# Depthwise convolution of the query tiles: from quad passes, VectorE and GpSimd taps to one phase-split pass on TensorE

## The reference

```python
# layer 0: linear attention over q, k, v and a second set of them out of two grouped convolutions
qkv = concat(h @ wq.T, h @ wk.T, h @ wv.T)             # 768 channels
dw = conv(qkv, dw_kernel, 5x5, one filter per channel)  # depthwise, SAME
pw = conv(dw, pw_kernel, 1x1, groups of 8 channels)
f = concat(qkv, pw) as heads of 3 x 8 channels          # query, key, value
query, key = relu(f[q]), relu(f[k])
scores = einsum(value with a row of ones, key)          # summed over the pixels
out = einsum(scores, query); out = out[:-1] / (out[-1:] + EPS)
x = batchnorm(conv1x1(out, proj_kernel)) + x
# layer 1: softmax attention over 1024 pixels, keys and queries from the normalised image
x = conv1x1(softmax(F(norm x) . G(norm x)) @ H(x)) + x
```

## Time and profile before

| | before |
|---|---|
| median of 3 runs | 660.25 us (659.42 to 661.57) |
| profiled execution, its own time | 659.5 us |
| span, first to last instruction | 657.6 us |
| mean granted TensorE clock | 0.99 |
| PE, DVE, POOL, ACT busy | 617.1, 523.6, 494.3, 473.5 us |

### The profile page before, as it was taken

How to read it: one execution, slowest core, us unless ns; L and a number is a source line. 1 busy time by engine, 2 the same in 40 slices (tenths; PEclk the granted TensorE clock), 3 DMA queues, 4 the chain that set the end, 5 groups by cost and what they waited for, 6 DMA issues and landing times.

```text
span 657.6 us, 13133 instructions
## 1 busy us (share of the span) xinstructions
PE 617.1 (94%) x5448; PEld 445.1 (68%) x5448; DVE 523.6 (80%) x616; ACT 473.5 (72%) x772; POOL 494.3 (75%) x236
## 2 busy tenths in 40 slices
PE   5979989989899999999899999999999999899997
PEld 3845466647678876556578876557568875367897
DVE  4999895878869798977789999879889996264543
ACT  4698689877759798987786988888777786243331
POOL 4579879976998999977999899959989997013000
PEclk9989999999999999999999999999989999999999
DMA  8000000101100000001100000000100000000000
GB/s 318 9 1 4 2 2 2 64 2 64 65 1 17 21 30 1 1 2 64 65 1 17 16 18 17 3 1 1 65 0 17 16 18 18 0 1 1 16 17 33
DMA packets 6698, 16.67 MB, mean 25 GB/s; under 512 B 880, under 2 KB 1136, under 8 KB 6128
## 3 DMA queue, kind: packets, MB, share of 16 engines
q1 hardware_dynamic: 6640, 15.84, 6.7%
HBM read 11.64 MB, written 4.19 MB: 24 GB/s over the span
## 4 chain that ended last, share of the span: by engine, by line
PE 80%; DVE 11%; ACT 5%; issue 2%; DMA 1%; SPq 0%; DVEq 0%; ACTq 0%
PE ps L786 12%; PE ps L762 12%; PE ps L597 7%; PE ps L877 5%; PE ps L531 5%; PE ps L535 4%; PE ps L532 4%; PE ps L777 4%; DVE ps L1365 3%; PE ps L843 2%; PE ps L635 2%; PE ps L810 2%; PE ps L731 2%; PE ps L605 2%; DVE small L1545 2%
## 5 line engine op out<-in xcount | busy, mean ns | idle before, releaser
L1626 POOL TENSOR_TENSOR conv<-conv,prod 128x930 f32<-128x930 f32 (+4 forms) x174 | 382.1, 2239 | 48.3 <-ACT prod L1068 45.5
L1365 DVE SCALAR_TENSOR_TENSOR ps<-raw,dw_sb,ps 128x930 f32<-128x930 f32 (+4 forms) x264 | 317.2, 1202 | 6.5
L1068 ACT ACTIVATE prod<-raw,dw_sb 128x961 f32<-128x961 f32 (+4 forms) x209 | 217.2, 1100 | 0.7 <-POOL q_raw L1626 0.7
L786 PE MATMUL ps<-ht,pt 128*128 128x256 f32 x384 | 86.4, 379 | 0.0
L1255 ACT ACTIVATE rows<-ps,small 128x1024 f32<-128x1024 f32 x32 | 35.7, 1115 | 69.2 <-DVE small L1550 69.1
L786 PEld LDWEIGHTS ps<-ht,pt 128*128 128x128 f32 x384 | 71.3, 190 | 8.9
L1626 POOL TENSOR_TENSOR rows<-rows,prod 128x930 f32<-128x930 f32 (+4 forms) x26 | 58.2, 2240 | 7.5 <-ACT prod L1068 4.3
L1545 DVE TENSOR_REDUCE small<-ps 128x1 f32<-128x1024 f32 x32 | 39.1, 1222 | 20.3 <-PE ps L762 20.3
L762 PE MATMUL ps<-hi,t_hi 128*128 128x512 f32 x128 | 45.3, 436 | 5.0 <-ACT rows L1255 5.0
L762 PE MATMUL ps<-lo,t_hi 128*128 128x512 f32 x128 | 41.2, 404 | 0.0
L531 PE MATMUL ps<-hi,wqkv_hi 128*128 128x512 f32 x92 | 38.7, 421 | 2.3 <-ACT t_sums L1099 1.5
(11 more groups left out here) (185 smaller groups left out, 1163.2 us busy)
## 6 DMA issues: line engine op xcount, KB each, us to landing
q_raw<-x_dram SPq DMA_DIRECT2D x8, 512.0 KB, 5.4
x<-x_dram SPq DMA_DIRECT2D x4, 1024.0 KB, 4.7
out_dram<-x_t SPq DMA_DIRECT2D x16, 256.0 KB, 2.0
conv<-wqkv_dram SPq DMA_DIRECT2D x1, 768.0 KB, 4.3
conv<-fg_dram SPq DMA_DIRECT2D x1, 512.0 KB, 5.9
proj_sb<-proj_dram SPq DMA_DIRECT2D x1, 512.0 KB, 7.4
pw_sb<-pw_dram SPq DMA_DIRECT2D x1, 384.0 KB, 6.6
mask_sb<-masks_dram SPq DMA_DIRECT2D x1, 280.0 KB, 6.2
```

Source lines behind the costliest of these rows:

```text
L786: mm = pe.matmul(dst[:, 0:C], pt[:, i % PT_BUFS, j, :], ht[:, j, :], start=(j == 0), stop=(j == NB - 1))
L1068: act.activation(dst, view, ACT.Copy, scale=weight(t, i)).then_inc(prod_ready, 1)
L1365: return dve.scalar_tensor_tensor(dst, view, w, before, ALU.mult, ALU.add)
L1626: pool.tensor_tensor(total, total, product, ALU.add).then_inc(conv_pool, 1)
```

## The change

The two query tiles leave DVE, ACT and POOL: their depthwise convolution is done whole on PE, in one pass an image, `phase_conv`. The image is split into four phases (even and odd rows by even and odd columns) of 16 x 16 pixels with a border of one. A 5x5 filter over the image is, phase by phase, a sum over nine offsets of the phase images. 8 channels x 4 phases make the 32 rows of a tile, so one 32*32 weight does all taps of one offset for 8 channels and all four output phases; four channel groups (`g`) are the column groups and four units (`r`) the row groups. A wave is sixteen 32*32 matmuls with 256 columns; there are 2 tiles x 9 offsets = 18 waves, and both tiles' sums share the four banks.

ACT writes the raw queries into `stage` by phase (two copies of 256 elements in place of one of 512). Sixteen DMAs move them so that the phases of a channel lie in neighbouring partitions (`load_phases`, SBUF to SBUF, 32 partitions x 2 pieces each), into the place where `t_hi` and `t_lo` lie later; the tables of the weights lie beside them and in `pt` and are loaded again for each image (`load_taps`). For the next image `phase_conv` stands behind `output_weights(b, 1)`; for image 0 in the prologue between the two spreads of the denominators. ACT's `phase_sums` empties the four banks. The pointwise step of the queries is by phase: for each of four units eight 128*32 matmuls with 256 columns, and ACT's relu puts the pixels back in order. `shared_quads`, `first_quads(2)` and `(3)`, the lates, POOL's part of tile 1, DVE's taps of tile 0 and the weight products for tiles 0 and 1 go. `PROD_BUFS` is 4 and the `TAPS_` and `PRODUCTS_` tables, `RSTD_AT` (where POOL's two powers stand among the adds) and the tables of the prologue have new numbers.

```diff
-LATE_OF = (9, 10, 10, 10)
-SHARED_OF = (0, 3, 3, 3)
-QUAD_OF = (16, 12, 12, 12)
-FIRST_QUAD_TAPS = 12
-PROD_BUFS = 5
+LATE_OF = (0, 0, 0, 0)
+SHARED_OF = (0, 0, 0, 0)
+PHASES = 4
+PSIDE = SIDE // 2 + 2
+PIMG = PSIDE * PSIDE
+OFFSETS = [(ey, ex) for ey in (-1, 0, 1) for ex in (-1, 0, 1)]
+PROD_BUFS = 4
...
-    return own + [(SHARED_TILE, i) for i in SHARED_REST[b][LATE_OF[b] + SHARED_OF[b]:]]
+    return [(t, i) for t in (2, 3) for i in TAP_RANGE]
...
-TAPS_PROJ = ((1, 0, 1, 0, 1, 0, 1, 1), (1, 0, 1, 0, 1, 0, 0, 0), (1, 0, 1, 0, 1, 0, 1, 1))
-TAPS_STAT = (1, 0, 0)
+TAPS_PROJ = ((1, 0, 1, 0, 1, 0, 0, 7), (1, 0, 0, 0, 0, 0, 0, 6), (1, 0, 0, 0, 0, 0, 1, 5))
+TAPS_STAT = (3, 4, 1)
...
-FIRST_SPLIT = 24
+FIRST_SPLIT = 19
...
-            a_end = lay_out(A_AT, [("sums_0", QUADS), ("pwkv", A_PWKV), ("sums_1", QUADS)], b_, a_end)
+            a_end = lay_out(A_AT, [("pwkv", A_PWKV)], b_, a_end)
...
-            a_end = lay_out(A_AT, [("mb_raw", nx)], b_ + 1, a_end)
+            a_end = lay_out(A_AT, [("mb_raw", nx), ("sums", QUADS * nx)], b_ + 1, a_end)
...
+            def load_taps():
+                for t in range(CK):
+                    sp.dma_start(tap_weights[t], taps_phases[t]).then_inc(taps_loaded, 16)
+
+            def load_phases(b):
+                sp.wait_ge(a_free, A_RQ[b][-1] + 1)
+                for f in range(PHASES):
+                    for g in range(QUADS):
+                        sp.dma_start(phased[f::PHASES, :, g, :], stage[g::QUADS, :, f, :]).then_inc(phases_loaded, 16)
...
             for b in range(B):
+                if b + 1 < B:
+                    if b == 0:
+                        sp.wait_ge(a_full, A_AT["sums", 0] + QUADS)
+                    load_taps()
+                    load_phases(b + 1)
                 if b + 2 < B:
                     sp.wait_ge(d_full, D_AT["proj", b] + D_PROJ)
                     load_x(b + 2)
...
+            def phase_conv(b):
+
+                pe.wait_ge(taps_loaded, 16 * CK * (b + 1))
+                pe.wait_ge(phases_loaded, 16 * PHASES * QUADS * (b + 1))
+                for t in range(CK):
+                    for e, (ey, ex) in enumerate(OFFSETS):
+                        for r in range(QUADS):
+                            k = slice(r * QUAD, (r + 1) * QUAD)
+                            bank = a_slot(A_AT["sums", b] + r) if t == e == 0 else a_bank(A_AT["sums", b] + r)
+                            for g in range(QUADS):
+                                view = phased_img[k, t, g, 1 + ey:PSIDE - 1 + ey, 1 + ex:PSIDE - 1 + ex]
+                                mm = pe.matmul(bank[g * QUAD:(g + 1) * QUAD, t * QUARTER:(t + 1) * QUARTER],
+                                               tap_weights[t][k, e, g, :], view,
+                                               start=(e == 0), stop=(e == len(OFFSETS) - 1))
+                mm.then_inc(a_full, QUADS)
...
+                dst = a_slot(A_AT["pwq", b] + 2 * t + h)
+                if t == h == 0:
+                    pe.wait_ge(pw_phases_loaded, 16)
+                    pe.wait_ge(a_free, A_AT["sums", b] + QUADS)
+                for x in range(2):
+                    for r in range(QUADS):
+                        mm = pe.matmul(dst[r * QUAD:(r + 1) * QUAD, x * QUARTER:(x + 1) * QUARTER],
+                                       pw_ph[:, t, r, 2 * h + x, :], conv_ph[:, t, r, :], start=True, stop=True)
                 mm.then_inc(a_full, 1)
...
             def body(b):
                 with_next = b + 1 < B
-                shared_quads(b, 0)
...
-                shared_quads(b, 1)
                 if with_next:
                     raw_kv(b + 1)
...
                 output_weights(b, 1)
+                if with_next:
+                    phase_conv(b + 1)
...
-            first_quads(2)
             first_whole(1)
             fused_weights(A_AT["mb_raw", 0], A_AT["st_raw", 0], 0)
             spread_denominators(D_AT["bc_raw", 0], 1, 0)
-            first_quads(3)
+            phase_conv(0)
...
+                    for y in range(2):
+                        mm = act.copy(stage_img[:, t, 2 * y:2 * y + 2, rows_at, 1:PSIDE - 1],
+                                      src.rearrange("p (a y c x) -> p y x a c", y=2, c=SIDE // 2, x=2)[:, y])
...
+            def phase_sums(b):
+
+                slot = A_AT["sums", b]
+                act.wait_ge(a_full, slot + QUADS)
+                for r in range(QUADS):
+                    act.copy(conv_ph[:, :, r, :], a_bank(slot + r).rearrange("p (t n) -> p t n", t=CK)).then_inc(a_free, 1)
...
                     fused_weights(A_AT["mb_raw", b + 1], 0)
+                    phase_sums(b + 1)
                 x1_transposes(b, 3)
...
-                    pool.wait_ge(d_full, D_AT["proj", b] + D_PROJ)
-                    quad_products(pool, later_weights, SHARED_TILE, QUAD_OF[b + 1]).then_inc(quad_weights_ready, 1)
```

More of the change, by code:

```diff
@@ L75 @@
 CARRY = (0, 0, 0, 0)
[L78 to L82, removed]
+LATE_SEQ = [[] for _ in range(B)]
 def pool_order(b):
[L87 to L90, removed]
+    return [(t, i) for i in TAP_RANGE for t in (POOL_TILES if b else FIRST_POOL_TILES)]
 def dve_order(b):
-    own = [(t, i) for t in (2, 3, 0) for i in TAP_RANGE if b or t or i not in FIRST_QUAD_SEQ]
-    return own + [(SHARED_TILE, i) for i in SHARED_REST[b][LATE_OF[b] + SHARED_OF[b]:]]
+    return [(t, i) for t in (2, 3) for i in TAP_RANGE]
 POOL_SEQ = [pool_order(b) for b in range(B)]
 DVE_SEQ = [dve_order(b) for b in range(B)]
-POOL_STARTS = [[(t, 0) for t in POOL_TILES] + SHARED_SEQ[b][:1] for b in range(B)]
+POOL_STARTS = [[(t, 0) for t in POOL_TILES] for b in range(B)]
 ADD_SEQ = [[tap for tap in POOL_SEQ[b] if tap not in POOL_STARTS[b]] for b in range(B)]
@@ L141 @@
[L141 to L147, removed]
@@ L611, in first_quads @@
                 t, h = QUAD_UNITS[n]
[L612 to L613 removed]
+                quads(A_AT[f"first_{n}", 0], t, h, list(TAP_RANGE), first_weights)
             def first_whole(h):
@@ L619, in first_whole @@
                 whole(dst, lambda r: quad_ident, h, True).then_inc(a_full, 1)
-            def shared_quads(b, h):
-                pe.wait_ge(a_free, A_RQ[b][-1] + 1)
-                pe.wait_ge(quad_weights_ready, b + 1)
-                quads(A_AT[f"sums_{h}", b], SHARED_TILE, h, QUAD_SEQ[b], later_weights if b else first_weights[SHARED_TILE])
-            def queries(b, t, h):
-                dst, cols, late = a_slot(A_AT["pwq", b] + 2 * t + h), slice(h * HALF, (h + 1) * HALF), t == SHARED_TILE
-                own = any(tap[0] == t for tap in DVE_SEQ[b] + POOL_SEQ[b])
-                last = [tap for tap in DVE_SEQ[b] if tap[0] == t][-1:]
-                if h == 0 and last:
-                    pe.wait_ge(conv_dve, dve_count(b, DVE_SEQ[b].index(last[0]) + 1))
-                if own:
-                    mm = pe.matmul(dst, pw_sb[:, t, :], conv[:, t, cols], start=True, stop=(b > 0 and not late))
-                if late and LATE_SEQ[b]:
-                    if h == 0:
-                        pe.wait_ge(conv_pool, late_add_count(b, late_adds_of(b)))
-                    pe.matmul(dst, pw_sb[:, t, :], late_of[b][:, cols], start=not own, stop=False)
-                if late or b == 0:
-                    if h == 0 and not late:
-                        pe.wait_ge(pw_quads_loaded, 16)
-                    pe.wait_ge(a_free, (A_AT[f"sums_{h}", b] if late else A_AT[f"first_{2 + h}", b]) + QUADS)
-                    mm = whole(dst, lambda r: pw_quad[:, t, r, :], h + (2 if late and b == 0 else 0),
-                               not own and not (late and LATE_SEQ[b]))
@@ L842, in body @@
                         if t < 2 * CK:
-                            pe.matmul(dst[:, c0:c0 + P], block, pw_sb[:, t, :], start=True, stop=True)
+                            pe.matmul(dst[:, c0:c0 + P], block, pw_sb[:, t - CK, :], start=True, stop=True)
                         else:
@@ L1381, in conv_taps @@
                     before = None if starts else acc
-                    if t == SHARED_TILE and starts and SHARED_OF[b]:
-                        before = final
-                        dve.wait_ge(conv_pool, add_count(b, len(ADD_SEQ[b])))
                     tap(final if i == NTAPS - 1 else acc, t, i, before).then_inc(conv_dve, 1)
```

152 lines of the change are left out of this document (89 added, 63 removed).

## The result

| | before | after |
|---|---|---|
| median | 660.33 us (4 runs, 659.42 to 661.57) | 671.01 us (4 runs, 667.36 to 672.43) |
| ratio | | 1.0169 [1.0144, 1.0194] |
| profiled execution / its span | 659.5 / 657.6 us | 667.36 / 665.6 us |
| mean granted TensorE clock | 0.99 | 0.976 |

The forecast was 651, the range 641 to 668.

What follows compares the result with a forecast made beforehand. PE's own sequence was taken as the bound: 659.5 - 5.8 - 26.6 (quad passes) - 15.0 (queries) + 38.4 (three later phase_convs) = 650.5, so 651 us as the median against 660.25; range 641 to 668.

Steps and rivals of the forecast that it cites:

- Instruction supply: In phase_conv: 100 matmul records and loads a us, near the quads' 64, so instruction fetches cost nothing in the sum.
- Both signs of being wrong: Listed among the signs of a wrong forecast: phase_conv over 13.8 us, and gaps with "issue" inside it.
- a mis-sized term: phase_conv's 18 waves at 0.64 us each, 11.5 us a call, with 8.0 and 11.9 at the ends.
- The start of image 0's pointwise step: L843 in image 0, at 86.16 before: taken as unchanged, with PE back near 75.0 + 11.5 = 86.5.
- The quad passes: Shared tile's passes on PE's path, removed: 5.8 us saved in image 0, 26.6 in images 1 to 3.
- the queries of image 0: Pointwise step of the queries: four units in 4.0 us for 8.2 before, 4.2 us saved in image 0.
- the phases were in time: Sixteen DMAs of load_phases before phase_conv: costed at nothing, the phases being wanted 27 us after the last query row.
- Starvation of POOL: Behind phase_conv: 2.5 us of POOL idle, hidden as long as POOL has the room of the removed adds.
- all else: Quad passes and queries of images 1 to 3, beyond image 0: PE gives up 37.4 us.
- Fetch stalls: Rival, chance 0.13: each phase_conv crosses 4.6 fetches at 0.86 us, growing by 4.0 us; 16 in four images, 667.
- Paced by their count: Rival, chance 0.08: tile matmuls cost 31 ns a record whatever their columns, phase_conv 18.0 us, 677 in all.
- The other rivals: POOL late for L843 (0.10, 658.7); relief of DVE, POOL and ACT pays (0.09, 644); phases land late (0.04, 666).

Runs made afterwards that it cites:

- e1: The changed kernel with half the columns in every matmul of phase_conv and as many instructions (part of the convolution left out): 675.93 us.
- e3: The changed kernel with the fold's spread and last two fused weights moved inside the later phase_convs, ACT's fold and DVE's taps moved too: 657.23 us, 0.9982 to before.
- e7: The changed kernel with five of nine offsets in phase_conv, ten waves in place of eighteen (convolution not whole): 644.82 us.
- e2: The changed kernel with four of ACT's five products among image 0's raw queries moved behind them: 670.09 us, ratio 1.0178 to before.
- e6: The changed kernel with prologue edits alone: products behind raw queries, denominators' scores after 34 DVE taps for 39, second spread inside phase_conv(0): 666.80 us, 1.0133 to before.

## Why the prediction was wrong

**The step that failed** is "Instruction supply ... I value this at nothing in the sum". It chose the right suspect (the waits in L656) and argued it away by an average rate: phase_conv's 100 instructions a us were called nearer to the quads' 64 than to the 197 of L656. The limit lies between them: one block of 256 in 3.45 us is 74 a us. At the quads' 31 ns a record the 128 matmul records of a block take 4.0 us, an estimate from the earlier trace rows, so the next block is there in time. Those of phase_conv take 2.74 us. The first block end in each call passes freely, 8 to 21 us after the one before it, since slower work lies between; at 13 of the 15 that follow, PE stops, and a round then takes 3.28 to 3.73 us. Both signs of being wrong that the prediction named for this came: a phase_conv over 13.8 us and "issue" inside it. The fetches and the places of the stops show the cause, e1 and e3 that neither the columns nor the records' number alone sets the time, and e7 that fewer blocks mean fewer stops.

**The size.** phase_conv was put at 11.5 us and measured 15.06 on average. Unstalled, four waves take 2.74 us, 0.685 a wave where 0.64 was taken: 18 x 0.685 = 12.3, and e3 measures 12.3. That is 0.8 over, a mis-sized term; the other 2.7 come with the supply, 2.3 of them as idle time with "issue" (9.0 over the four calls). Four times 3.56 is 14.2 of the 17.0 us.

The Trainium skill's page "Runtime: NRT & Kernel Launch", section "Instruction fetch mechanics", gives blocks of 256 instructions, and the distance of the stops agrees; that the fetch is mostly hidden, as it says, doesn't hold here, by 0.24 to 0.98 us at each stop.

**The start of image 0's pointwise step** was taken as unchanged, and was 5.7 us later. phase_conv(0) took 3.7 more than its 11.5, and the second spread, 1.6 us from 90.22 to 91.82, stands behind it: the prediction's step counted one spread where the kernel has two. The last 0.4 are its own 86.5 beside 86.16. Nothing of the 5.7 is hidden: e7 shows that the cover, DVE's taps, ends at 84.74.

That phase_conv(0) started at 75.02 is luck. The prediction kept the spread at 73.52, but a quad pass stood ahead of it that goes:

```profile
66.62 4.17 PE L597 MATMUL ps<-raw,ht 32*32 32x512 f32 x96
```

From 66.62 to the next step at 71.46, 4.8 us were given up there. As much came back ahead of it: the first quads start 1.8 us later (e2) and take 9.35 us for 7.00, at a granted clock of 0.50 from 46.8 to 53.7, and the next pass and the stop in the scores are longer. In e2 and e6 the start is 74.60 and 72.61.

**What held.** The quad passes are gone, the queries of image 0 take 3.66 us against 4.0, the wait of 0.77 behind phase_conv came, the phases were in time (2.0 us from issue to landing, and no wait for them at 151.92), and PE never waited for POOL. Starvation of POOL was larger than thought and cost nothing:

```profile
170.79 2.29 POOL L1648 TENSOR_TENSOR conv<-conv,prod 128x992 f32<-128x992 f32 x1 [12.06 <-ACT prod L1087]
```

12.06 us of idle in place of 2.5, since ACT stood 14.88 us before phase_sums, with the removed adds as its cover.

**The smaller differences.** Stops came and went elsewhere, as a block's end fell into a dense run of small matmuls or not: the 2.00 us in image 0's L656 are gone, and 0.93 and 1.72 appeared in the queries of images 2 and 3, at the same place of their blocks. They are 2.65, or 2.1 beside a stop of 0.51 in before's image 3 that went, where 1.9 are to be explained in "all else".

The forecast had no term for the granted clock. It stood at the lower of its two levels, 1.2 GHz, for 31.6 us of after's span and for 13.7 of before's; behind the prologue it is 21.4 and 10.2. At half speed the 11 us more cost up to 5.6, an estimate. In after it fell at 91.2, 169.7 and 323.3, each time 1 to 3 us behind the end of a phase_conv and for 3.4 us, but not behind that of image 3, and in e3 not behind that of image 0. The pointwise step of image 0 took 1.3 us longer for it (granted clock 0.80 from 91.8 to 98.8 us; 1.00 before; 5.59 us in e3). Why it fell stays open. The four phase_convs ran at 1.00, so their price stands without it.

**Rivals.** "Fetch stalls" (667, chance 0.13) is what happened and for its reason, at 2.7 us a phase_conv against its 4.0: 13 stops of 0.69 us, where it counted 4.6 of 0.86 in each call. That its 667 lies so near the measured time is in part luck, since the longer waves and the second spread add what the stops lack. "Paced by their count" is wrong as a pace of the records, for 128 of them started in 1.89 us in e1, 15 ns each; it looks alike because supply is a price by count. The other rivals show no trace. Why the medians lie 10.7 us apart and the profiled executions 7.9 stays open: the profile is that of the lowest (granted clock 0.976; 0.974 and 0.975 in the others).

## What to carry to other kernels

Many small matmuls on tiles of the array trade columns for instructions, so price them twice: by columns, and by instructions (matmul records and weight loads) against the supply, here one block of 256 in about 3.45 us. A dense stretch that runs through whole blocks faster than that is best cut by sparse work that has to be done anyway, so that one block in two lasts longer than a round; here the work inserted at 256 and 416 records took the stops away, and at 544, behind the last of them, it did not. And a piece put "between" two steps on the engine that bounds costs what stands behind it as well: count the sequence up to the next wait, not the piece alone.

## What the hardware showed that was not expected

- All 95 stops inside phase_conv, in the nine kernels that have it, stand at the end of a block of 256 of PE's instructions, and PE goes on 1.2 to 1.6 us after a 16 KB fetch on the instruction queue has landed.
- In the dense stretch the next fetch starts about 1.1 us after PE has entered the block before. A round takes 3.45 us in most cases and 3.73 in many others, with 128 columns as with 256, and in e1 also where the records ran at half clock.
- 128 tile matmuls of 256 columns take 2.74 us, 21 ns a record, where one such record alone would stream in about 0.22 by the prediction's figure: some ten side by side, an estimate.
- 94 us of work taken off POOL and 104 off DVE left no gain that these traces show outside the stages whose own PE work changed.
